# AdaLN block with two attention stages on one core: eight steps of 20 unit-matrix turns on TensorE are taken out of the head

## The reference

```python
mod = (_silu(L0_c) @ L0_wmod).reshape(L0_c.shape[0], 6, 1, -1)
sa, ca, ga, sb, cb, gb = (mod[:, k] for k in range(6))
ga = (2 * (ga >= 0) - 1) * jnp.maximum(jnp.abs(ga), 0.25)      # gb likewise
h = _layernorm(x, axis=-1) * (1 + ca) + sa
x = x + ga * _L0_attn_ref(h, guidance_trajectories)            # mean over the last 8 differences, with a softmax over 64 guides
h = _layernorm(x, axis=-1) * (1 + cb) + sb
x = x + gb * _L0_ffn_ref(h, wqkv, q_scale, k_scale, wo, ln_g, ln_b, w1, b1, w2, b2)
```

## Time and profile before

| what | value |
|---|---|
| median of three executions | 829.01 us |
| the profiled execution's own time | 828.6 us |
| its span, first to last instruction | 826.8 us |
| busy: PE, DVE, ACT, POOL | 739.7, 642.8, 651.9, 560.0 us |
| mean granted TensorE clock | 0.990 of full speed |
| turns of L871, all between 16.3 and 79.7 us | 160, 0.27 us each from start to end |

### The profile page before, as it was taken

How to read it: one execution, slowest core, us unless ns; L and a number is a source line. 1 busy time by engine, 2 the same in 40 slices (tenths; PEclk the granted TensorE clock), 3 DMA queues, 4 the chain that set the end, 5 groups by cost and what they waited for, 6 DMA issues and landing times.

```text
span 826.8 us, 20278 instructions
## 1 busy us (share of the span) xinstructions
PE 739.7 (89%) x7391; PEld 544.2 (66%) x7391; DVE 642.8 (78%) x1575; ACT 651.9 (79%) x1543; POOL 560.0 (68%) x428
## 2 busy tenths in 40 slices
...
PEclk9999999999999999999999999999999999999996
...
DMA packets 12713, 10.05 MB, mean 12 GB/s; under 512 B 1088, under 2 KB 11720, under 8 KB 12616
## 3 DMA queue, kind: packets, MB, share of 16 engines
...
## 4 chain that ended last, share of the span: by engine, by line
PE 37%; ACT 19%; POOL 19%; issue 12%; DVE 12%; DMA 1%; POOLq 0%; SPq 0%; ACTq 0%; DVEq 0%
ACT probs L1148 7%; PE pair L842 6%; POOL qk L1713 6%; POOL roots L1658 5%; PE dense L997 4%; PE mixed L888 4%; POOL qk L1704 3%; ACT probs_t L1156 3%; PE pair L928 2%; PE dense L988 2%; PE dense L985 2%; PE dense L1079 2%; PE dense L986 2%; PE dense L1082 2%; PE mixed L953 1%
## 5 line engine op out<-in xcount | busy, mean ns | idle before, releaser
L1658 POOL TENSOR_TENSOR roots<-powers,minus_half 128x16 f32<-128x16 f32 (+1 forms) x65 | 191.9, 2952 | 5.3
L1713 POOL TENSOR_TENSOR qk<-qk,turned_s 128x512 f32<-128x512 f32 x128 | 168.1, 1330 | 7.4 <-DVE turned_s L1592 5.4
L1148 ACT ACTIVATE probs<-pair,neg_max 128x128 f32<-128x128 f32 x512 | 139.2, 410 | 9.2 <-DVE neg_max L1409 8.5
L1592 DVE TENSOR_TENSOR turned_s<-dense,tables 128x512 f32<-128x512 f32 x128 | 87.5, 683 | 24.5 <-ACT qk L1273 22.9
L1079 PE MATMUL dense<-wq_hi,h_hi 128*128 128x512 f32 x192 | 90.3, 470 | 15.0 <-DVE turned_s L1592 7.6
L1704 POOL TENSOR_TENSOR qk<-qk,tables 128x512 f32<-128x512 f32 x64 | 83.1, 1302 | 29.4 <-ACT qk L1273 29.3
L1409 DVE TENSOR_REDUCE neg_max<-pair 128x4 f32<-128x512 f32 x128 | 81.1, 683 | 22.6 <-PE pair L928 22.3
L1269 ACT ACTIVATE squares<-dense 128x512 f32<-128x512 f32 x128 | 78.5, 615 | 19.0 <-PE dense L1082 13.7
L842 PE MATMUL pair<-eye_s,probs 128*128 128x128 f32 x512 | 76.0, 279 | 14.3 <-ACT probs L1148 13.9
L1597 DVE TENSOR_REDUCE powers<-squares 128x8 f32<-128x512 f32 x128 | 86.5, 676 | 0.0
L1391 DVE TENSOR_TENSOR qk<-qk,roots 128x1024 f32<-128x1024 f32 x64 | 82.3, 1287 | 1.0 <-POOL roots L1658 1.0
...
## 6 DMA issues: line engine op xcount, KB each, us to landing
...
```

Of the source, the lines that this page charges most:

```text
L1148: last = act.activation(probs[:, ring, hh, :], banks[m][:, hh * P:(hh + 1) * P], ACT.Exp, bias=neg_max[:, ring, hh:hh + 1], scale=1.0)
L1592: dve.tensor_tensor(turned_s[:, t % 2, m, :].rearrange("p (h a b) -> p h a b", h=HEADS, a=2), halves[:, :, ::-1, :], rot(layer, t, 2 * m + 1),
L1658: return pool.tensor_tensor(to, of, minus_half[0:of.shape[0], 0:of.shape[-1]], ALU.pow)
L1713: pool.tensor_tensor(part, part, turned_s[:, t % 2, m, :], ALU.add).then_inc(added, 1)
```

## The change

The eight words `-1/3:setup.warm.0` to `-1/3:setup.warm.7` are taken out of TensorE's list. The function that would run them stays, unused. The lists of ACT, DVE and POOL, SyncE's queue, and the banks of every step are what they were. The text of the list is wrapped anew, so the diff shows many lines; these are the first of them:

```diff
--- before.py
+++ after.py
@@ -47,46 +47,44 @@
...
 
 ORDER = {
     "pe": steps("""
-        -1/3:setup.silu -1/3:setup.mod -1/3:new.turn -1/3:setup.guide -1/3:new.dots -1/3:setup.warm.0
-        -1/3:setup.gate -1/3:new.mix -1/3:new.sum -1/3:setup.rows -1/3:setup.warm.1 -1/3:setup.warm.2
-        -1/3:new.stream -1/3:setup.warm.3 0/2:new.turn 0/2:proj.tile.0.0 0/2:proj.tile.0.1 0/2:proj.tile.0.2
-        0/2:proj.tile.1.0 0/2:proj.tile.1.1 0/2:proj.tile.1.2 0/2:new.dots 0/2:proj.tile.2.0 -1/3:setup.warm.4
-        -1/3:setup.warm.5 -1/3:setup.warm.6 0/2:proj.tile.2.1 0/2:new.mix 0/2:proj.tile.3.0 0/3:a.turn.0.0
-        0/2:new.sum 0/2:proj.tile.3.2 0/3:a.turn.0.1 0/3:a.turn.1.1 0/3:a.turn.1.0 0/2:proj.tile.2.2
-        0/2:proj.tile.3.1 0/3:a.score.0 0/3:a.score.1 0/3:a.flip.0.0 0/2:new.stream 0/3:a.flip.0.1 -1/3:setup.warm.7
...
+        -1/3:setup.silu -1/3:setup.mod -1/3:new.turn -1/3:setup.guide -1/3:new.dots -1/3:setup.gate -1/3:new.mix
+        -1/3:new.sum -1/3:setup.rows -1/3:new.stream 0/2:new.turn 0/2:proj.tile.0.0 0/2:proj.tile.0.1
+        0/2:proj.tile.0.2 0/2:proj.tile.1.0 0/2:proj.tile.1.1 0/2:proj.tile.1.2 0/2:new.dots 0/2:proj.tile.2.0
+        0/2:proj.tile.2.1 0/2:new.mix 0/2:proj.tile.3.0 0/3:a.turn.0.0 0/2:new.sum 0/2:proj.tile.3.2 0/3:a.turn.0.1
+        0/3:a.turn.1.1 0/3:a.turn.1.0 0/2:proj.tile.2.2 0/2:proj.tile.3.1 0/3:a.score.0 0/3:a.score.1 0/3:a.flip.0.0
+        0/2:new.stream 0/3:a.flip.0.1 0/3:a.mix.0.0 0/3:a.mix.0.1 0/3:proj.tile.0.0 0/3:proj.tile.2.2 0/3:a.flip.1.0
...
```

More of the change, by code:

```diff
@@ L55 @@
-        0/2:new.sum 0/2:proj.tile.3.2 0/3:a.turn.0.1 0/3:a.turn.1.1 0/3:a.turn.1.0 0/2:proj.tile.2.2
-        0/2:proj.tile.3.1 0/3:a.score.0 0/3:a.score.1 0/3:a.flip.0.0 0/2:new.stream 0/3:a.flip.0.1 -1/3:setup.warm.7
-        0/3:a.mix.0.0 0/3:a.mix.0.1 0/3:proj.tile.0.0 0/3:proj.tile.2.2 0/3:a.flip.1.0 0/3:a.out.0 0/3:a.flip.1.1
-        0/3:a.turn.2.1 0/3:proj.tile.0.1 0/3:a.mix.1.0 0/3:a.mix.1.1 0/3:proj.tile.1.0 0/3:proj.tile.1.1
-        0/3:proj.tile.2.0 0/3:proj.tile.0.2 0/3:a.turn.2.0 0/3:new.turn 0/3:proj.tile.1.2 0/3:a.out.1
@@ new lines @@
+        0/3:a.out.0 0/3:a.flip.1.1 0/3:a.turn.2.1 0/3:proj.tile.0.1 0/3:a.mix.1.0 0/3:a.mix.1.1 0/3:proj.tile.1.0
+        0/3:proj.tile.1.1 0/3:proj.tile.2.0 0/3:proj.tile.0.2 0/3:a.turn.2.0 0/3:new.turn 0/3:proj.tile.1.2
+        0/3:a.out.1 0/3:proj.tile.2.1 0/3:a.turn.3.1 0/3:new.dots 0/3:proj.tile.3.0 0/3:a.turn.3.0 0/3:a.score.2
+        0/3:a.score.3 0/3:a.flip.2.0 0/3:proj.tile.3.1 0/3:a.flip.2.1 0/3:a.flip.3.0 0/3:new.mix 0/3:a.flip.3.1
+        0/3:a.mix.2.0 0/3:a.mix.2.1 0/3:a.mix.3.0 0/3:a.mix.3.1 0/3:a.out.2 0/3:new.sum 0/3:a.out.3 1/0:a.turn.0.1
@@ new lines @@
+        1/0:a.turn.1.1 1/0:a.turn.0.0 1/0:a.turn.1.0 0/3:a.project 1/0:a.score.0 1/0:a.score.1 1/0:ff.stats
+        0/3:proj.tile.3.2 1/0:a.flip.0.0 1/0:a.flip.0.1 1/0:a.flip.1.0 1/0:a.flip.1.1 1/0:a.mix.0.0 1/0:a.mix.0.1
+        1/0:ff.norm 0/3:new.stream 1/0:a.mix.1.0 1/0:a.mix.1.1 1/0:a.out.0 1/0:ff.up.0.0 1/0:a.out.1 1/0:ff.up.1.0
+        1/0:ff.up.1.1 1/0:ff.up.0.1 1/0:a.turn.2.1 1/0:a.turn.3.1 1/0:a.turn.2.0 1/0:ff.up.2.0 1/0:ff.up.2.1
+        1/0:ff.down.0 1/0:ff.down.1 1/0:ff.down.2 1/0:a.turn.3.0 1/0:a.score.2 1/0:a.score.3 1/0:proj.tile.0.0
@@ new lines @@
+        1/0:a.flip.2.0 1/0:proj.tile.0.1 1/0:proj.tile.1.0 1/0:a.flip.2.1 1/0:a.flip.3.0 1/0:proj.tile.1.1
+        1/0:proj.tile.0.2 1/0:a.flip.3.1 1/0:proj.tile.1.2 1/0:a.mix.2.0 1/0:a.mix.2.1 1/0:proj.tile.2.0
+        1/0:a.mix.3.0 1/0:a.mix.3.1 1/0:proj.tile.2.1 1/0:proj.tile.3.0 1/0:proj.tile.3.1 1/0:a.out.2 1/0:a.out.3
+        1/0:proj.tile.3.2 1/0:a.project 1/1:a.turn.0.1 1/1:a.turn.0.0 1/1:a.turn.1.0 1/1:a.turn.1.1 1/1:a.score.0
+        1/1:a.score.1 1/1:ff.stats 1/0:proj.tile.2.2 1/1:a.flip.0.0 1/1:a.flip.0.1 1/1:a.flip.1.0 1/1:a.flip.1.1
@@ new lines @@
+        1/1:a.mix.0.0 1/1:a.mix.0.1 1/1:ff.norm 1/1:a.mix.1.0 1/1:a.mix.1.1 1/1:a.out.0 1/1:a.turn.2.1 1/1:ff.up.0.0
+        1/1:ff.up.1.0 1/1:ff.up.1.1 1/1:ff.up.0.1 1/1:ff.up.2.1 1/1:ff.up.2.0 1/1:ff.down.0 1/1:ff.down.1
+        1/1:ff.down.2 1/1:a.out.1 1/1:a.turn.2.0 1/2:new.turn 1/1:a.turn.3.1 1/1:a.score.2 1/1:proj.tile.0.0
+        1/1:proj.tile.0.1 1/1:proj.tile.1.2 1/1:a.turn.3.0 1/1:proj.tile.1.0 1/1:a.flip.2.0 1/1:proj.tile.1.1
+        1/1:proj.tile.2.0 1/1:a.flip.2.1 1/1:proj.tile.3.0 1/1:proj.tile.2.1 1/1:a.score.3 1/1:proj.tile.0.2
@@ new lines @@
+        1/1:proj.tile.3.1 1/1:a.mix.2.0 1/1:proj.tile.2.2 1/1:a.mix.2.1 1/1:proj.tile.3.2 1/2:new.dots
+        1/1:a.flip.3.0 1/1:a.flip.3.1 1/1:a.mix.3.0 1/1:a.mix.3.1 1/2:a.turn.0.1 1/1:a.out.2 1/1:a.out.3
+        1/2:proj.tile.0.0 1/2:a.turn.0.0 1/2:a.turn.1.0 1/2:a.turn.1.1 1/2:a.score.0 1/2:a.score.1 1/1:a.project
+        1/2:a.flip.0.0 1/2:proj.tile.0.2 1/2:a.flip.0.1 1/2:a.flip.1.0 1/2:proj.tile.0.1 1/2:a.flip.1.1
+        1/2:a.mix.0.0 1/2:a.mix.0.1 1/2:proj.tile.1.0 1/2:a.mix.1.0 1/2:a.mix.1.1 1/2:a.turn.2.1 1/2:a.out.0
```

7 lines of the change are left out of this document (added).

## The result

| | median | range | executions |
|---|---|---|---|
| changed kernel | 834.27 us | 832.74 to 835.78 | 7 |
| kernel before, beside it | 829.11 us | 828.74 to 831.36 | 7 |

The ratio of the two is 1.0057, with a 95% interval of 1.0044 to 1.0071. The change makes the kernel slower by 0.6%, 5.2 us. The profiled execution of the changed kernel took 832.74 us, the shortest of its seven; that of the kernel before took 828.6. So the two profiles stand 4.1 us apart, and the medians one more.

What follows compares the result with a forecast made beforehand. The first 80 us were taken as a chain from engine to engine, whose losses reach the end. A 0, B 1.5, C 2.5 and D 0.7 sum to 4.7 us: 833.3 profiled, 833.7 us median, forecast 832 to 836, range 829.8 to 838.

Steps and rivals of the forecast that it cites:

- As work the turns cost nothing: All 160 turns: each is covered by other waits, so removing them as work saves 0.1 us at most.
- A: Pause behind the gates: half clock slows `new.mix` and `new.sum`, but VectorE takes the sum only at 34.20; 0, bound 1.5 us.
- B: `new.stream` and first projections: half clock at 40.72 makes ScalarE's copy of tile 1.0 late; 1.5 us, bounds 0.45 and 2.3.
- C: Hole of 60 turns ahead of tile 2.1: half clock there, all let through to the end; 2.5 us, bounds 0 and 3.4.
- D: First `a.mix`: pause grows to 2.76 us, the clock falls half the time; 0.7 us, bounds 0 and 2.9.
- Behind 80 us nothing: Rest of the kernel: nothing changed and no clock fall seen before the last slice, so nothing added.
- rival 1: The clock stays away longer: B 2.3, C 3.4, A 1.5, D 2; +9 us, 838; chance 0.12.
- Rival 2: It hardly matters: transposes did not hold the clock, or the next engines cover the loss; 828 to 830.5; chance 0.11.
- Rival 3: Only part: clock back after 4 us at most in B and C; B 0.9, C 1.3; 831 us; chance 0.13.
- Rival 4: Not slower: without `warm.3` the second unit's turn comes up to 2.35 us earlier; 826.7 us; chance 0.04.

Runs made afterwards that it cites:

- e4: Kernel before without only the 20 turns ahead of the first `a.mix` (`warm.7`): 830.65 us against 829.81, ratio 1.0011.
- e10: Kernel before with only the first 20 of the 60 turns in the hole ahead of tile 2.1 kept: 831.36 us against 830.12, ratio 1.0020.
- e11: Kernel before with 40 of the 60 turns in the hole ahead of tile 2.1 kept: 830.84 us against 830.12, ratio 1.0008.
- e7: Kernel before with turns added at the start, 8 ahead of `setup.mod` and 15 ahead of `new.dots`: 828.59 us against 829.66, ratio 0.9985.
- e3: Kernel before without only the 20 turns ahead of the gates (`warm.0`): 831.42 us against 829.81, ratio 1.0016.
- e2: Kernel before without only the 60 turns around `new.stream` (`warm.1` to `warm.3`): 831.95 us against 829.81, ratio 1.0018.
- e1: Kernel before without only the 60 turns between projections 2.0 and 2.1 (`warm.4` to `warm.6`): 831.53 us against 829.81, ratio 1.0021.
- e5: Kernel before with its turns done by matmuls instead of transposes, `WARM_TURNS` 10 instead of 20: 829.84 us against 829.66, ratio 1.0003.
- e8: Kernel before with the added turns of both e6 and e7: 827.01 us against 829.66, ratio 0.9961.
- e6: Kernel before with turns added in the tail, 34 behind `4/3:ff.stats` and 8 behind `4/3:ff.norm`: 827.27 us against 829.66, ratio 0.9976.

## Why the prediction was right, and where it was off

The forecast was 833.7 us for the median and 833.3 for the profiled execution; 834.27 and 832.74 were measured.

Two readings of the prediction are off, and nothing rests on them. A mean clock of 0.72 over half a microsecond is 0.22 us at full and 0.28 at half, so the fall lies at 35.22 us and not at 35.28. And GpSimd does pause between its additions, for 0.49 us ahead of 51.54.

The steps of the prediction, with lags taken from VectorE:

**As work the turns cost nothing.** Held. No place got earlier: from the first loads on the lag never falls below +0.14 us.

**A, the pause after the gates: 0.** Held in the profile, in size and in its reason. The pause grew to 4.73 us, half clock began at 26.0, `new.mix` started at 26.36 and ran until 29.2, `new.sum` ended at 32.9, and VectorE took it at 34.35 against 34.20, the 0.14 with which it came. The clock was back after 3.0 us of work, sooner than the 4.1 to 5.8 assumed. And the premise that `warm.0` keeps the clock up here holds only at times: in e4 and e10, which keep it, the clock falls too. In e11 it then stays at half until 37.1 us, and `new.sum`, ending at 34.19, costs 0.2 us with `warm.0` in place. e7 shows the price where that slack is gone, 1.0 us of the bound of 1.5. e3's median says that taking `warm.0` out still costs 1.3 us in a way that its profile doesn't show; this part of A, 0.16 of the whole 0.57%, is open.

**B, `new.stream` and the first projections: 1.5.** Measured 1.53 - 0.14 = 1.39. `h_hi` came 0.45 late of its own, the first matmul of tile 1.0 at 49.33 where I had 49.06, and GpSimd's addition at 53.07 instead of 51.54. The clock was back at 49.8, within the 48.8 to 51.9 given. Alone, in e2, it shows 0.8, with the clock back 1.9 us sooner; whether B needs `warm.0` out too to come to 1.4 was not separated.

**C, the hole of 60 turns: 2.5.** Tile 2.1 started 1.53 us late and at half clock, which stayed for 4.8 us of work (4.1 to 5.8 foreseen). VectorE's L1592 came 3.65 - 1.53 = 2.1 us later than it would have; its wait for ScalarE's `qk` grew from 0.87 to 2.99 us. That is the low end of the price on TensorE. But 0.8 of it was back by 79 us. Three instructions of VectorE got shorter: L1391 1.21 instead of 1.48 us, L1435 0.17 instead of 0.73, L1439 with its four 1.76 instead of 2.05; that is 1.1 us, of which 0.8 shows in the lag. What differs is what GpSimd did beside them. Before, L1435 ended at 73.18, and GpSimd's L1704, which was running when it started, at 73.16; in the changed kernel GpSimd was idle beside it, waiting for it. GpSimd's own small instruction behind the additions, beside VectorE's L1391 before, took 1.22 us then and 0.25 after. Timeline of VectorE and GpSimd before:

```profile
67.31 1.48 DVE L1391 TENSOR_TENSOR qk<-qk,roots 128x1024 f32<-128x1024 f32 x1
...
72.45 0.73 DVE L1435 TENSOR_SCALAR power_n_first<-mean_var_first 128x4 f32<-128x4 f32 x1
...
74.31 2.05 DVE L1439 TENSOR_SCALAR y_t<-x_in,mean_var_first,root_n_first 128x128 f32<-128x128 f32 x4
```

```profile
67.69 1.22 POOL L1664 TENSOR_SCALAR powers<-powers 128x16 f32<-128x16 f32 x1
...
71.89 1.27 POOL L1704 TENSOR_TENSOR qk<-qk,tables 128x512 f32<-128x512 f32 x1
```

and in the changed kernel:

```profile
70.97 1.21 DVE L1389 TENSOR_TENSOR qk<-qk,roots 128x1024 f32<-128x1024 f32 x1
...
75.83 0.17 DVE L1433 TENSOR_SCALAR power_n_first<-mean_var_first 128x4 f32<-128x4 f32 x1
...
77.41 1.76 DVE L1437 TENSOR_SCALAR y_t<-x_in,mean_var_first,root_n_first 128x128 f32<-128x128 f32 x4
```

```profile
69.19 0.25 POOL L1662 TENSOR_SCALAR powers<-powers 128x16 f32<-128x16 f32 x1
...
76.08 1.01 POOL L1656 TENSOR_TENSOR root_n_first<-power_n_first,minus_half 128x4 f32<-128x4 f32 x1 [2.39 <-DVE power_n_first L1433]
```

Net C is 1.3 us. I had let the whole of it through and looked only at what waits for TensorE, not at what VectorE's own work costs beside GpSimd's. In e1 it is 2.6 and then 1.8.

**D, the first `a.mix`: 0.7.** The clock did fall, at 84.0 and thus behind the `a.mix` of 82.92: its pause was 2.59 us. 1.3 us were lost by 86 and 0.5 were left at 96. The size was right, and e4 shows the same (1.2 and then 0.5). `a.mix` itself was 2.8 us late and not 4, since C was smaller.

**Behind 80 us nothing.** Wrong. The lag grows from 3.4 at 96 us to 4.2 at the end, 0.32 of it at 268 us, where VectorE waits for a load. And the clock falls behind 76 us in the profiles of many kernels whose order there is that of before: around 77 us in e5, e8 and e11, around 106 in e1, e2, e6, e7 and e10, around 381 in e6, e7 and e8. At 106 and 381 each fall costs 1.2 to 1.3 us, at 77 less: 0.5 us in e5 (lag -0.21 at 76, +0.26 at 100) and 0.15 in e8 and in e11. Over 35 executions of the kernel before, the mean clock runs from 0.982 to 0.990 and the time against it has a correlation of -0.72: 1 us for each 0.004. The profile from which I argued, at 0.990, was one of the best of them. The chance falls, which one profile can't show, go with about half of that scatter (0.72 squared is 0.52). The profiled execution of the changed kernel had the highest clock of its seven, 0.976. On average the changed kernel has 0.969 and the kernel before 0.986: the gap, 0.017, is somewhat wider than the 0.014 between the two profiles, as the medians are 5.2 us apart and the profiles 4.1. That the falls behind 80 us come more often with turns taken out would fit, but no profile shows it.

So the sum, for the profiled pair: 0.14 + 0 + 1.39 + 2.12 - 0.83 + 0.54 + 0.81 = 4.17 us, where 4.7 was foreseen as 0 + 1.5 + 2.5 + 0.7. That total came out close because two errors, C too high and nothing behind 80 us, cancelled. That is luck, and so is the median: it came within 0.6 us of the forecast with a part in it, e3's, that the sum has at 0.

**The rivals.** Of rival 1 the condition came about in part: half clock lasted from before 40.85 to 49.8, 9.0 us from the first work, but 5.0 from the first projection at 44.84. It priced this at 2.3 for B and the next engines took only 1.4. Rival 2 fell in both halves: e5 shows that transposes count, and the lags show that the loss reached the other engines. Rival 3 has for C the size that was measured net (1.3), for another reason: the clock was not back sooner, VectorE regained it. Rival 4 fell; nothing came earlier.
